# Layer 1's graph visits: products with zeros between TensorE's sums, and lane numbers read from SBUF

## The chip, the cores and the metric

One core of one Trainium2 chip runs the whole program. The metric is the time of one execution in microseconds on the device; the time before is the median of three runs.

## The reference

Two layers of a graph network over 6250 nodes of 256 features and 100000 edges, sorted by their target node `dst`. Layer 1, in which the change lies, computes a graph attention. The core of it, for edges with row = `src` and col = `dst`:

```python
h = (x @ W).reshape(n, 4, 64)
e = leaky_relu((a_l * h).sum(-1)[row] + (a_r * h).sum(-1)[col], 0.2)
ex = exp(e - segment_max(e, row)[row])
att = ex / segment_sum(ex, row)[row]
out = segment_sum(att[:, :, None] * h[col], row)      # (n, 256)
```

Around it stand layer norms, a linear attention and a mixture of experts, which the change does not touch.

## The kernel before

The nodes are tiled by 128 (49 tiles). The edges, sorted by the node that they are summed into, are cut into chunks of 128; a *visit* is one chunk for one tile of nodes. Layer 1 has 880 visits in 110 groups of eight (U = 8). The code is unrolled, with an own list of instructions for each engine; semaphores alone order them.

For each visit POOL gathers 128 rows of `h1_table` (264 numbers each) with one indirect DMA (L534). There are R = 4 slots of eight visits; before each half group of four, POOL waits until PE has summed the visits whose slot it refills (`gnn_ps`). For a group g, in this order:

- DVE compares lane numbers with the node of each edge (`one_hot`, L2088, 128 x 1024, into bf16); the lane numbers of all groups but the first two come from PSUM bank 7 (`lanes_ps`), into which L2131 copied them from `iota`.
- PE transposes the eight one-hots into bank 0 (`flip_hot`, L2168), ACT copies them out (L2037), PE looks up the numbers of the target nodes with them (`look_up`, L2177). ACT widens the one-hots to float32 (L2041).
- DVE makes the scores in four short steps (`attend` stages 0 to 3, the last L2109), ACT takes the exponential (L2045, L2046), DVE multiplies the gathered rows by it in two halves (stages 5 and 6, L2120).
- PE multiplies the one-hot of each visit with its rows (L2196, 128 x 260 float32, banks 4 to 6 in turn) and DVE adds the bank to the tile's sum in SBUF (`add_sums`, L548). PE's sum of visit n waits until DVE has added visit n - 3.

The program order ties the groups together. DVE does the eight adds of group g and, behind each of the last seven, one stage of group g + 1. PE does the look-ups of g + 1, then the sums of g, with the transposes of g + 2 between the fourth and the fifth sum. ACT does the exponentials of g + 1, the copy of the transposed one-hots of g + 2, and widens those of g + 2 when the sums of g are over.

`zeros` is a 128 x 128 float32 tile of zeros in SBUF that other stages use already; `xres` holds the residual of all nodes.

In layer 0, the stretches 440 to 780 and 840 to 1400 us below run visits of their own (gather L534, sum L1216 of 256 columns, add L548) beside other work of PE, DVE and ACT.

Of the kernel before, what the change touches and what calls it, by code (L numbers as in the profile page):

```python
# [16 lines left out]
P = 128  # L17
NODES, D, EDGES = 6250, 256, 100000
# [86 lines left out]
def gps_two_layers(nc, x, src, dst, edge_weight, L0_gnn_W, L0_gnn_b, L0_mix_Wq, L0_mix_Wkv, L0_mix_Wproj,  # L105
# [4 lines left out]
    with ExitStack() as ctx:  # L110
        def sem(name):
            return ctx.enter_context(nc.semaphore(name))
# [18 lines left out]
        def take(words):  # L131
            at = place["at"]
            place["at"] = at + words
            assert place["at"] <= place.get("end", arena_words), place
            return arena[:, at:at + words]
# [4 lines left out]
        xres = take(T * D)  # L140
        ident, tri, ones, iota = take(P), take(P), take(P), take(P)
        zeros, no_edges = take(P), take(2 * SPAN)
# [26 lines left out]
        def bank(b, width=512, at=0):  # L169
            return ps[:, b * 512 + at:b * 512 + at + width]  # L170

        def half(b, i, width=D):
            return ps[:, b * 512 + i * 256:b * 512 + i * 256 + width]

        V, G = Steps(nc.vector, sem("dve_step")), Steps(nc.gpsimd, sem("pool_step"))
# [361 lines left out]
        def load_tiles(engine, first):  # L537

            return nc.values_load_multi_w_load_instructions(
                tile_row[0:1, ds(first, U)], engines=[engine.engine], min_val=0, max_val=T,  # L540
                skip_runtime_bounds_check_because="a visit's tile is a count of at most T tiles")[1]

        def add_sums(dve, n, tile, width, b, sums_before, adds_before):

            dve.wait_ge(gnn_ps, n + (sums_before + 1))
            dve.wait_ge(gnn_add, n + adds_before)
            to = acc[:, ds(tile * ACC_W, width)]
            dve.tensor_tensor(to, to, bank(b, width), ALU.add).then_inc(gnn_add, 1)  # L548
# [1452 lines left out]
        scratch(FREE)  # L2001
        hot = take(2 * U * P).rearrange("p (b u n) -> p b u n", b=2, u=U)
        assert place["at"] <= arena_words - KD * P - SLOT_W
        lanes_ps = bank(7, P)
        ex_ps = bank(1, U * GH).rearrange("p (u h) -> p u h", u=U)
        lc3 = lc.rearrange("p (t w) -> p t w", w=2 * GH)
        rl3 = rl_all.rearrange("p (t w) -> p t w", w=2 * GH)
# [12 lines left out]
        with nc.Block() as block:  # L2020
# [42 lines left out]
            @block.vector  # L2063
            def _(dve):

                V.then(dve.tensor_reduce(r_max, rl3[:, 0:T, 0:GH].rearrange("p t h -> p h t"), AX_X, ALU.max))
                dve.tensor_copy(r_rows.rearrange("p (h n) -> p h n", h=GH),
                                r_max.unsqueeze(2).to_broadcast([P, GH, P])).then_inc(rm_done, 1)
                dve.wait_ge(rm_ps, 1)
                V.then(dve.tensor_reduce(r_max, bank(7, GH * P).rearrange("p (h n) -> p h n", h=GH), AX_X, ALU.max))  # L2070
                dve.sem_inc(rm_done, 1)
                V.then(dve.memset(lc, 0.0))
                V.add(dve.tensor_copy(lc3[:, 0:T, 0:GH], rl3[:, 0:T, GH:]))
                bound = lc3[:, 0:T, GH:]
                V.then(dve.tensor_tensor(bound, rl3[:, 0:T, GH:], r_max.unsqueeze(1).to_broadcast([P, T, GH]), ALU.add))
                V.then(dve.scalar_tensor_tensor(bound, bound, ALPHA, bound, ALU.mult, ALU.max))
                V.then(dve.tensor_scalar(bound, bound, -LIFT - OTHER, None, ALU.add))
                for q in range(PARTS):
                    V.then(dve.tensor_copy(lcp[:, :, q, :], lc3))
                    if q + 1 < PARTS:  # L2080
                        V.then(dve.tensor_tensor(lc3, lc3, lcp[:, :, q, :], ALU.subtract))
                V.then(dve.tensor_copy(ident_b, ident))
                dve.sem_inc(lc_done, 1)
                dve.sem_inc(gnn_add, GNN1_BANKS)

                def one_hot(g, b, lanes):
                    wide = [P, U, P]
                    dve.tensor_tensor(hot_b[b].rearrange("p (u n) -> p u n", u=U), lanes.unsqueeze(1).to_broadcast(wide),  # L2088
                                      v_loc[:, ds(g * U, U)].unsqueeze(2).to_broadcast(wide), ALU.is_equal
                                      ).then_inc(hots_done, 1)  # L2090

                def attend(g, stage):

                    r, b = g % R, g % 2
                    if stage == 0:
                        dve.wait_ge(rows_done[r], g // R * (16 * U) + (ROWS_BEFORE[r] + 16 * U))
                        dve.wait_ge(look_ps, g + 1)
                        V.add(dve.tensor_reduce(look, bank(2 + b, U * LW).rearrange(
                            "p (u q w) -> p u w q", u=U, q=PARTS), AX_X, ALU.add))
                    elif stage == 1:  # L2100
                        V.settle()
                        V.add(dve.tensor_tensor(score, look[:, :, 0:GH], rows[r][:, :, D:D + GH], ALU.add))
                    elif stage == 2:
                        V.settle()
                        V.add(dve.scalar_tensor_tensor(score, score, ALPHA, score, ALU.mult, ALU.max))
                    elif stage == 3:
                        V.settle()

                        dve.scalar_tensor_tensor(score, look[:, :, GH:], OTHER, score, ALU.add, ALU.subtract  # L2109
                                                 ).then_inc(score_done, 1)  # L2110
                    elif stage == 4:
                        if g + 2 < GROUPS1:
                            dve.wait_ge(hot_done32, g + 1)
                            one_hot(g + 2, b, lanes_ps)
                    else:
                        dve.wait_ge(ex_done, g + 1)
                        q = (stage - 5) * HALF_U
                        msg = rows[r][:, q:q + HALF_U, 0:D].rearrange("p u (h f) -> p u h f", h=GH)
                        ex = ex_ps[:, q:q + HALF_U, :].unsqueeze(3).to_broadcast([P, HALF_U, GH, GF])
                        dve.tensor_tensor(msg, msg, ex, ALU.mult).then_inc(msg_done, 1)  # L2120

                STAGES = 7

                for g in range(2):
                    one_hot(g, g, iota)
                for c in range(LOOPS):
                    dve.wait_ge(mx_ps, c + 1)
                    a = xres[:, c * B * D:(c + 1) * B * D]
                    dve.tensor_tensor(a, a, half(4 * (c % 2), 0, B * D), ALU.add).then_inc(mx_add, 1)
                dve.wait_ge(mx_add, LOOPS)  # L2130
                V.then(dve.tensor_copy(lanes_ps, iota))  # L2131
                dve.wait_ge(edges_ready, 2)
                for stage in range(STAGES):
                    attend(0, stage)
                for g in range(GROUPS1):
                    tiles = load_tiles(dve, g * U)
                    for u in range(U):
                        add_sums(dve, g * U + u, tiles[u], ACC_W, 4 + (g * U + u) % GNN1_BANKS, SUMS_BEFORE + R * U,
                                 ADDS_BEFORE + GNN1_BANKS)
                        if u >= U - STAGES and g + 1 < GROUPS1:  # L2140
                            attend(g + 1, u - (U - STAGES))
                dve.wait_ge(gnn_add, NVIS + NVIS1 + GNN0_BANKS + GNN1_BANKS)

            @block.tensor
            def _(pe):
# [4 lines left out]
                for c in range(LOOPS):  # L2150
# [4 lines left out]
                    for n, i in enumerate(group_tiles(c)):  # L2155
                        for k in range(KD):
                            last = pe.matmul(half(4 * (c % 2), n)[:, k * P:(k + 1) * P],
                                             xt_tile(i)[:, k * P:(k + 1) * P], kvm[:, k * P:(k + 1) * P],
                                             start=True, stop=True)
# [24 lines left out]
                for g in range(GROUPS1):  # L2184
                    r, b = g % R, g % 2
                    if g + 1 < GROUPS1:
                        look_up(g + 1, 1 - b)
                    pe.wait_ge(hot_done32, g + 1)
                    pe.wait_ge(den_in, g + 1)
                    for u in range(U):  # L2190
                        if u % HALF_U == 0:
                            pe.wait_ge(msg_done, g * 2 + (u // HALF_U + 1))
                        if u == HALF_U and g + 2 < GROUPS1:
                            flip_hot(g + 2, b)
                        pe.wait_ge(gnn_add, g * U + (ADDS_BEFORE + u + 1))
                        pe.matmul(bank(4 + (g * U + u) % GNN1_BANKS, ACC_W), hot[:, b, u, :], rows[r][:, u, 0:ACC_W],  # L2196
                                  start=True, stop=True).then_inc(gnn_ps, 1)


        W_E = KD * F1  # L2200
# [641 lines left out]
```

## Time and profile before

| what | us |
|---|---|
| median of 3 runs | 4209.23 |
| lowest and highest run | 4208.39, 4214.93 |
| span of the profiled execution, first to last instruction | 4207.4 |
| TensorE's mean granted clock, share of full speed | 0.776 |
| the visits of layer 1, from about | 2107 |
| to about | 3462 |

No other time of the profiled execution is recorded than its span. Engines are named as in the profile: PE is TensorE, PEld its weight loads, DVE VectorE, ACT ScalarE, POOL GpSimd. A matmul on float32 data shows as two records, each with its weight load. PEclk is the clock granted to PE as a share of full speed, 1.0 for 2.4 GHz and 0.5 for 1.2 GHz. "issue" is time in which an engine waited for nothing that the profile shows, and "remote" stands for a releaser that it can't assign to an instruction.

### The profile page before, as it was taken

What the parts mean: (1) busy time and instruction counts of PE and PEld (TensorE: products, weight loads), DVE (VectorE), ACT (ScalarE), POOL (GpSimd) and SP (SyncE); (2) the same over time, 40 slices, a digit from 0 to 9 for tenths busy, and PEclk for the clock granted to TensorE, in tenths of its full rate; (3) what the DMA queues carried; (4) which work ended last, traced back from release to release, by engine and by line L of the source; (5) the groups of instructions that cost most, each with busy time, mean ns of one, the idle gap of its engine ahead of it and who ended that gap; (6) DMA issues with size and microseconds to landing.
All of it is one profiled execution on the core that took longest, in us unless ns stands there. A gap on an engine that the chain in (4) does not pass through costs nothing. (4 is left out here: it accounts for less than half of the span.)

```text
span 4207.4 us, 47856 instructions
## 1 busy us (share of the span) xinstructions
PE 2730.2 (65%) x12850; PEld 2053.4 (49%) x12850; DVE 2571.9 (61%) x5963; ACT 1421.0 (34%) x4306; POOL 2199.0 (52%) x2162
## 2 busy tenths in 40 slices
PE   5476777577777653815666666666666655699984
PEld 4243444355555543614544444444444435599972
DVE  5346998677777786435455565556555567544438
ACT  6663000077777731113221111111111113333334
POOL 0466777666666602573256665666665641255530
PEclk9778887788989865957777777777777775699985
DMA  5332333233333223622223333333333354222234
GB/s 145 87 87 82 89 88 87 86 87 93 89 93 95 86 67 87 159 62 66 69 78 86 91 87 85 87 89 89 89 87 86 87 79 159 76 72 70 71 92 145
DMA packets 204009, 379.38 MB, mean 90 GB/s; under 512 B 48926, under 2 KB 131873, under 8 KB 203619
## 3 DMA queue, kind: packets, MB, share of 16 engines
q0 software_dynamic: 102192, 279.12, 24.7%
q1 hardware_dynamic: 101556, 97.19, 7.5%
q8 instruction: 113, 1.85, 0.2%
q14 instruction: 148, 1.21, 0.1%
HBM read 314.12 MB, written 62.05 MB: 89 GB/s over the span
## 5 line engine op out<-in xcount | busy, mean ns | idle before, releaser
L534 POOL DMA_INDIRECT arena<-h_table,arena x1712 | 1729.3, 1010 | 1082.5 <-issue 479.2
L548 DVE TENSOR_TENSOR arena<-arena,ps 128x260 f32 (+1 forms) x1712 | 719.3, 420 | 848.1 <-remote 355.2
L2196 PE MATMUL ps<-arena 128*128 128x260 f32 x1760 | 674.2, 527 | 376.2 <-DVE arena L548 162.2
L1216 PE MATMUL ps<-arena 128*128 128x256 f32 x1664 | 556.6, 451 | 243.4 <-DVE arena L548 133.3
L2196 PEld LDWEIGHTS ps<-arena 128*128 128x128 f32 x1760 | 411.7, 258 | 534.5 <-issue 249.7
L1216 PEld LDWEIGHTS ps<-arena 128*128 128x128 f32 x1664 | 326.6, 221 | 400.1 <-issue 237.5
L717 ACT ACTIVATE arena<-arena 128x112 f16<-128x112 f16 x1568 | 446.7, 375 | 94.5 <-DVE arena L983 77.9
L2045 ACT ACTIVATE ps<-arena 128x32 f32<-128x32 f32 x110 | 22.1, 201 | 1036.9 <-DVE arena L2109 909.5
L884 DVE TENSOR_SCALAR arena<-arena 128x128 f32<-128x128 f32 x832 | 289.5, 349 | 0.4
L2120 DVE TENSOR_TENSOR arena<-arena,ps 128x1024 f32<-128x1024 f32 x220 | 267.1, 1214 | 2.1 <-ACT ps L2045 2.1
L2570 ACT ACTIVATE arena<-ps,arena 128x128 f32<-128x128 f32 x456 | 143.6, 366 | 307.1 <-PE ps L2618 274.6
L2618 PEld LDWEIGHTS ps<-arena 128*128 128x128 f32 x1824 | 222.8, 192 | 9.1 <-DVE arena L2577 3.4
L2618 PE MATMUL ps<-arena 128*128 128x128 f32 x1824 | 223.6, 276 | 2.6 <-DVE arena L2577 2.6
L2639 PE MATMUL ps<-arena 128*128 x912 | 215.6, 379 | 0.0
L580 ACT ACTIVATE arena<-arena 128x98 bf16<-128x98 f32 (+2 forms) x441 | 188.1, 432 | 77.4 <-remote 44.8
L2177 PE MATMUL ps<-arena 128*128 x880 | 128.6, 192 | 123.5 <-ACT arena L2037 76.8
L2266 POOL DMA_INDIRECT arena<-xn_table,arena x114 | 124.7, 1094 | 148.7 <-DVE arena L2492 101.1
L2557 POOL DMA_INDIRECT y_rows<-arena x114 | 114.8, 1007 | 163.5 <-DVE arena L2601 146.1
L1306 POOL DMA_INDIRECT arena<-xn_table,arena x84 | 81.4, 969 | 216.0 <-DVE arena L1559 160.3
L2177 PEld LDWEIGHTS ps<-arena 128*128 128x128 bf16 x880 | 88.6, 101 | 212.2 <-issue 183.9
L702 ACT ACTIVATE arena<-ps 128x256 f32<-128x256 f32 x98 | 37.3, 380 | 418.7 <-PE ps L1115 230.1
L2639 PEld LDWEIGHTS ps<-arena 128*128 128x128 f32 x912 | 164.5, 190 | 17.7
(525 smaller groups left out, 4486.5 us busy)
## 6 DMA issues: line engine op xcount, KB each, us to landing
arena<-h_table,arena POOLq DMA_INDIRECT x1712
arena<-in_L_ffn_w SPq DMA_DIRECT2D x32, 512.0 KB, 7.7
xn_table<-arena SPq DMA_DIRECT2D x14, 896.0 KB, 4.0
slot_out<-arena SPq DMA_DIRECT2D x21, 512.0 KB
arena<-y_rows SPq DMA_DIRECT2D x12, 896.0 KB, 9.5
h_table<-arena SPq DMA_DIRECT2D x7, 924.0 KB
h_table<-arena SPq DMA_DIRECT2D x7, 896.0 KB, 4.2
arena<-in_x SPq DMA_DIRECT2D x48, 128.0 KB
```

Of the source, the lines that this page charges most:

```text
L534: pool.indirect_dma_start(slot[:, 0:width], None, table, bass.IndirectOffsetOnAxis(ap=idx, axis=0)).then_inc(done, 16)
L548: dve.tensor_tensor(to, to, bank(b, width), ALU.add).then_inc(gnn_add, 1)
L580: act.activation(to, key, ACT.Sign, bias=edge_hi[:, b:b + 1], scale=-1.0, accum_out=out).then_inc(hist_done, 1)
L717: last = act.activation(codes[b][:, c, k, :], slots_[b][:, c, :], ACT.Copy, scale=code_f[k][:, at:at + 1])
L884: dve.tensor_scalar(hot_w[:, g % 2, u, :], iota, v_loc[:, n:n + 1], v_w[:, n:n + 1], ALU.is_equal, ALU.mult).then_inc(hot_done, 1)
L1216: pe.matmul(bank(n % V0_BANKS, D), hot_w[:, g % 2, u, :], rows[:, n % RING, :], start=True, stop=True).then_inc(gnn_ps, 1)
L2120: dve.tensor_tensor(msg, msg, ex, ALU.mult).then_inc(msg_done, 1)
L2177: last = pe.matmul(bank(2 + b, LW, u * LW), hot_t[:, u * P:(u + 1) * P], lc_parts[:, ds(tiles[u] * LW, LW)], start=True, stop=True)
L2196: pe.matmul(bank(4 + (g * U + u) % GNN1_BANKS, ACC_W), hot[:, b, u, :], rows[r][:, u, 0:ACC_W], start=True, stop=True).then_inc(gnn_ps, 1)
L2570: act.activation(h_t[b][:, f * P:(f + 1) * P], bank(2 + 2 * b + f // 2, P, f % 2 * P), ACT.Relu, bias=b1_t[:, ds(experts[b] * FB + f, 1)]) ...
L2618: last = pe.matmul(bank(2 + 2 * b + f // 2, P, f % 2 * P), w1_ring[b][:, k * F1 + f * P:k * F1 + (f + 1) * P], x_t[b][:, k * P:(k + 1) * P ...
L2639: last = pe.matmul(bank(6 + b, D), h_t[b][:, f * P:(f + 1) * P], w2_all[:, ds(experts[b] * W_E + f * D, D)], start=(f == 0), stop=(f == FB ...
```

## The change

Behind the sum of every visit of layer 1, PE gets one more product: `zeros` with the first 256 columns of `xres`, float32, into bank 7, without a wait and without a semaphore. Nobody reads the result. Since bank 7 held the lane numbers of `one_hot`, these are now read from `iota` in SBUF for all groups, and the copy into the bank goes.

```diff
-        lanes_ps = bank(7, P)
         ex_ps = bank(1, U * GH).rearrange("p (u h) -> p u h", u=U)
...
                         if g + 2 < GROUPS1:
                             dve.wait_ge(hot_done32, g + 1)
-                            one_hot(g + 2, b, lanes_ps)
+                            one_hot(g + 2, b, iota)
...
                 dve.wait_ge(mx_add, LOOPS)
-                V.then(dve.tensor_copy(lanes_ps, iota))
                 dve.wait_ge(edges_ready, 2)
...
                         pe.matmul(bank(4 + (g * U + u) % GNN1_BANKS, ACC_W), hot[:, b, u, :], rows[r][:, u, 0:ACC_W],
                                   start=True, stop=True).then_inc(gnn_ps, 1)
+                        pe.matmul(bank(7, D), zeros, xres[:, 0:D], start=True, stop=True)
```

## Rows read from the trace of the kernel before

**Rows 1.** The page: busy time of each engine over the whole span.

```profile
PE 2730.2 (65%) x12850; PEld 2053.4 (49%) x12850; DVE 2571.9 (61%) x5963; ACT 1421.0 (34%) x4306; POOL 2199.0 (52%) x2162
```

**Rows 2.** The last step of the softmax (L2109): times, first and last start.

```profile
L2109 DVE SCALAR_TENSOR_TENSOR arena<-arena x110: 185/186/247, 2108.2 to 3451.9; 128x32 f32<-128x32 f32 x110
```

**Rows 3.** Stretches: length, busy us (count) of PE, PEld, DVE, ACT, POOL, clock, DMA.

```profile
440.00:780.00 340.00, 242.28 (x692) 140.78 (x691) 297.20 (x676) 25.87 (x84) 270.77 (x228) 0.81 0.31 88
840.00:1400.00 560.00, 401.80 (x2149) 318.45 (x2148) 415.72 (x1107) 431.86 (x1516) 355.33 (x342) 0.88 0.32 91
2107.00:3436.00 1329.00, 834.34 (x3429) 563.91 (x3430) 767.22 (x1604) 241.45 (x429) 803.94 (x848) 0.72 0.34 87
```

**Rows 4.** Waits of 2107 to 3465: who, for whom, us, times, longest.

```profile
DVE arena L548 <- remote: 283.8, 75, 8.4
DVE arena L548 <- PE ps L2196: 211.2, 273, 2.9
DVE arena L548 <- issue: 40.3, 74, 7.3
...
POOL arena L534 <- PE ps L2196: 269.1, 110, 27.9
```

**Rows 5.** Timeline of DVE around a long wait: start, us, what, idle before.

```profile
2634.75 0.43 DVE L548 TENSOR_TENSOR arena<-arena,ps 128x260 f32 x1 [0.56 <-PE ps L2196]
...
2636.90 0.43 DVE L548 TENSOR_TENSOR arena<-arena,ps 128x260 f32 x1 [1.62 <-PE ps L2196]
...
2644.68 0.43 DVE L548 TENSOR_TENSOR arena<-arena,ps 128x260 f32 x1 [7.25 <-remote]
```

**Rows 6.** Timeline of PE in the same stretch.

```profile
2633.88 0.61 PE L2168 MATMUL ps<-arena 128*128 128x128 bf16 x8
2634.32 0.66 PE L2196 MATMUL ps<-arena 128*128 128x260 f32 x2
...
2637.38 0.71 PE L2196 MATMUL ps<-arena 128*128 128x260 f32 x2 [1.44 <-issue]
2645.16 1.24 PE L2196 MATMUL ps<-arena 128*128 128x260 f32 x2 [7.07 <-DVE arena L548]
```

**Rows 7.** Timeline of POOL there.

```profile
2641.29 0.95 POOL L534 DMA_INDIRECT arena<-h_table,arena  x1 [0.30 <-issue]
2647.19 0.94 POOL L534 DMA_INDIRECT arena<-h_table,arena  x1 [4.95 <-PE ps L2196]
```

**Rows 8.** Short stretches: behind another long wait, and the last two full groups.

```profile
2713.30:2717.50 4.20, 3.56 (x14) 2.89 (x15) 2.48 (x8) 0.00 (x0) 1.23 (x2) 0.50 0.01 2
...
3436.60:3444.40 7.80, 7.16 (x35) 4.59 (x33) 7.07 (x16) 2.30 (x4) 0.00 (x0) 0.86 0.38 34
3444.40:3451.90 7.50, 6.05 (x23) 4.31 (x23) 6.18 (x16) 2.19 (x4) 0.00 (x0) 0.81 0.00 0
```

**Rows 9.** Groups of instructions, 2000 to 3700: busy us, mean ns, idle before.

```profile
L2196 PE MATMUL ps<-arena 128*128 128x260 f32 x1760 | 674.2, 527 | 376.2 <-DVE arena L548 162.2 <-issue 157.8 <-DVE arena L2120 50.6
...
L2120 DVE TENSOR_TENSOR arena<-arena,ps 128x1024 f32<-128x1024 f32 x220 | 267.1, 1214 | 2.1 <-ACT ps L2045 2.1
L2088 DVE TENSOR_TENSOR arena<-ps,arena 128x1024 bf16<-128x1024 f32 x108 | 131.5, 1218 | 0.0
```

**Rows 10.** PE's sums back to back, at the full and at the half clock.

```profile
2703.46 0.82 PE L2196 MATMUL ps<-arena 128*128 128x260 f32 x3
...
2716.36 1.07 PE L2196 MATMUL ps<-arena 128*128 128x260 f32 x2
```

**Rows 11.** Single lines: ns shortest/median/longest.

```profile
L1216 PE MATMUL ps<-arena x466: 377/381/767, 440.5 to 779.9; 128*128 128x256 f32 x156
...
L2088 DVE TENSOR_TENSOR arena<-arena x2: 1222/1224/1226, 2054.8 to 2055.9; 128x1024 bf16<-128x1024 f32 x2
```

**Rows 12.** Timeline of the two comparisons with numbers from SBUF.

```profile
2054.75 2.37 DVE L2088 TENSOR_TENSOR arena<-arena 128x1024 bf16<-128x1024 f32 x2 [0.25 <-issue]
2055.63 1.17 POOL L534 DMA_INDIRECT arena<-h_table,arena  x1 [0.30 <-issue]
```

## The prediction

> **What bounds the kernel now.** I read the lanes of the page first, then the waits and the timeline of the stretch that the change touches. The page says that no engine is full over the span [rows 1], so the question is what sets the pace of this one stage, the 110 groups of eight visits in layer 1. The first step 3 of `attend` starts at 2108.2 us and the last at 3451.9 us [rows 2], so a group takes 1343.7 / 109 = 12.33 us. Against that stand the engines' own times. POOL needs 0.95 us for a gather and 0.30 us behind it [rows 7], 10.0 us for eight. From 2107 to 3436, 1329 us or 107.8 groups, DVE is busy 767.22 us, 7.1 us per group, and PE 834.34 us, 7.7 us [rows 3]. None fills 12.33 us. The waits tell where the rest goes: POOL waits 269.1 us for PE's sums, 2.45 us per group, and 10.0 + 2.45 is the group's time. It waits because its ring of four slots is full. DVE waits 283.8 us for something that the profile can't name ("remote"), in 75 pieces, 211.2 us for PE and 40.3 us for issue, 4.9 us per group together [rows 4].
>
> The 75 pieces decide. In the timeline [rows 5 to 7] the sum that PE starts at 2634.32, behind eight transposes, is over by 2634.98. DVE adds it at 2644.68, 9.7 us later, and has added nothing since 2637.33, while POOL goes on gathering until 2642.24. POOL then has nothing to do for 4.95 us until PE's sums free a slot. Where the gathers are over, in the last two full groups, the same instructions take 7.80 and 7.50 us [rows 8]. So a group is: DVE's own chain of about 7.5 to 8 us, and 4 to 5 us in which PE's finished work isn't seen by DVE, and this only while POOL gathers without a pause. The add at 2636.90 comes 2.15 us after the one before, the next 7.78 us later; the first step is one sum of two matmul records, the second eight transposes and a sum, ten records. That is 0.8 to 1.1 us for a record. It looks as if PE's work were reported one record at a time and slowly in these pieces, but the trace doesn't show why.
>
> The granted clock over the stage is 0.72 [rows 3], so PE is at the lower of its two levels for 2 x (1 - 0.72) = 56% of the time.
>
> **The change, part by part.** *The zero matmuls.* 880 more instructions in the code, one behind each sum, each of 256 float32 columns. A sum of 260 columns shows as two records (1760 for 880 visits [rows 9]), so there are 1760 more records and as many weight loads. The price is not in the trace of this stage, but its neighbour is: at the full clock three records in a row take 0.82 us, the last 0.38, so one starts 0.22 us after the other; at the half clock two take 1.07 us, the last 0.64, so 0.43 us [rows 10]. A record of 256 columns in layer 0 takes 377 ns at its shortest [rows 11], as good as the same. So a zero product costs 2 x 0.22 = 0.43 us at 2.4 GHz and 2 x 0.42 = 0.85 us at 1.2 GHz, 3.5 or 6.8 us for a group. PE idles 12.33 - 7.7 = 4.6 us per group, so the work fits at the full clock. What hides it is the time in which PE waits anyway for an add (three banks of sums, so PE is at most three sums ahead) and for DVE's two multiplications of 1.21 us at the end of the group [rows 9]. At the full clock a sum and its zeros, 0.87 us, are slower than DVE's add with a small step of the softmax, 0.43 + 0.19 us with their gaps, for sums 4 and 5 alone: some 0.1 to 0.3 us per group without cover.
>
> *Half clock behind a stall.* After such a piece PE stands at the lower level: at 2645.16 one pair takes 1.24 us [rows 6], and the clock from 2713.3 to 2717.5, behind another, is 0.50 [rows 8]. I count all 75. There a zero product of 0.85 us stands in the way of one sum or none before DVE's long operations cover it again: 0 to 0.85 us, I take the middle, 0.4 us x 75 = +30 us. The 0.1 to 0.3 us of the full clock I leave in the interpolation below, which contains it.
>
> *What the clock gives back.* More work between the sums makes the lower level rarer. DVE waits for PE 273 times [rows 4]. A sum at the full clock comes 0.43 us sooner. If the share at the lower level is halved, that is 273 x 0.43 x 0.28 = 33 us; bounds: nothing, and all 211.2 us.
>
> *The weights in front.* Each zero product loads `zeros`, and each sum after it its own one-hot again. The loads lie beside the matmuls: the three records at 0.22 us from start to start [rows 10] have a load in front of each. Nothing.
>
> *More records to report.* This is the term that I think decides. A group has 16 records of sums, 8 of transposes and 8 of look-ups, 32; with the change 48. If the "remote" time goes by records, it grows by half: 283.8 x 0.5 = +142 us, the upper bound. If it ends when POOL's ring is full whatever PE does, as at 2642.24, it stays: +0. Between them I go by three stretches with the same gathers and other numbers of PE records [rows 3]: layer 0 from 440 to 780 has 692 / 228 x 8 = 24 records for eight gathers and 340 / 228 = 1.49 us per gather; this stage 32 and 1329 / 848 = 1.57 us; layer 0 from 840 to 1400 has 50 and 560 / 342 = 1.64 us. From 32 to 48 that is 0.07 x 16 / 18 = 0.062 us per visit, x 880 = +55 us. The three differ in much else, so this is an estimate.
>
> *Lanes from SBUF.* 108 comparisons from the bank take 1218 ns [rows 9], the two from SBUF 1224 ns [rows 11]: 108 x 6 ns = +0.7 us, and one copy of 128 columns goes. The gather that began in the middle of those two took 1.17 instead of 0.95 us [rows 12]. At worst 0.22 us x 108 = 24 us of POOL, which has 269.1 us of waiting to hide it in; if that cover is gone, it shows in full. I take 0. The Trainium skill (SBUF — State Buffer, Who interferes with whom) says that a DVE instruction with two SBUF inputs contends with a GpSimd instruction that reads SBUF, and infers that descriptor generation isn't hit. By the stronger reading each comparison could hold POOL for its whole 1.2 us, 108 times; the row of 1.17 us allows a fifth of that.
>
> Sum: 55 + 30 - 33 = +52 us on a span of 4207.4 us. The span is the profiled execution's whole record; it lies 1.8 us below the median of the runs, 4209.23 us, so the prediction is 4261 us. A difference of 0.2%, 8 us, is what a measurement of this kernel can tell from none.
>
> **The rivals.** *The clock wins.* PE stays at the upper level, its sums are there when DVE asks, and the pieces without reports get shorter as PE never rests. For it: 162.2 + 157.8 us of idle time before PE's sums [rows 9], and the level 0.50 after a stall [rows 8]. Against: the stalls are 5 to 8 us of waiting that zeros between sums can't fill, since PE is three sums ahead and stops. The gain is half of DVE's 211.2 us, -105 us, 4104 us; with the whole of it and some of the remote time up to -200 us. It decides if the remote time doesn't grow with the records. The Trainium skill (TensorE: Matmul & The Clock Gate, HAM oscillation) says that gaps between matmul bursts bring the half clock back and that a kernel without them gains. By that rule alone the outcome would be this rival.
>
> *Nothing to see.* The zeros lie in PE's idle time, the remote time ends with POOL's ring, and POOL's 10.0 + 2.45 us stand: 4209 +- 8 us. For it speaks that POOL paces the group; against it that there are 16 new records between what DVE waits for.
>
> *PE becomes the bound.* At the lower level a group costs PE 8 x 0.86 us for sums, 6.8 for zeros and twice the 0.61 of the full clock for the transposes [rows 6], 14.9 us. If the lower level keeps its 56%, the loss is 0.56 x (14.9 - 12.33) x 110 = +158 us, 4367 us. Against it: PE that has been busy for a while gets the upper level back: transposes at the upper level stand at 2633.88 [rows 6] in the middle of a dense group, so the state ends itself.
>
> **How the numbers follow.** Forecast case 0.52 (4261 us, its own range 4222 to 4348: 30% of the 55 us give 16 + 30 - 33 = +13, the upper bound of the records gives 142 + 30 - 33 = +139). The clock wins 0.25, nothing 0.15, PE bound 0.08. The range is to leave out no more than the far end of the clock's gain, below 4120, and what lies above PE's bound, a tenth each at most: 4120 to 4370 us. Slower 0.52 + 0.08 = 0.60; same 0.15; faster 0.25.
>
> **What would show it.** Right: between two steps of the softmax 12.8 us on average; the new matmul with 1760 records; a granted clock above 0.8 in the stage and yet DVE's "remote" wait above 283.8 us; POOL's gathers still at 0.95 us. Wrong: "remote" smaller than before with a higher clock (the clock wins), or the same group time with PE busy 3.5 us more (nothing). If gathers take 1.1 us or more, the lanes in SBUF did it. If PE is busy over 11 us of a group at a clock near 0.6, PE is the bound.

## The result, and the profile after

The changed kernel takes 4337.56 us (median, 4333.24 to 4342.21), the kernel before beside it 4208.81: ratio 1.0311, interval 1.0291 to 1.0332, so 3.1% or 129 us slower. The forecast was slower by 52 us. The profiled execution took 4333.24 us with a span of 4331.5.

The page's busy line, and the last step of the softmax (L2108, which was L2109; shortest, median and longest ns, first and last start), after:

```profile
PE 3014.0 (70%) x14610; PEld 2381.7 (55%) x14610; DVE 2572.7 (59%) x5962; ACT 1425.8 (33%) x4306; POOL 2241.4 (52%) x2162
```

```profile
L2108 DVE SCALAR_TENSOR_TENSOR arena<-arena x110: 185/186/257, 2108.1 to 3573.2; 128x32 f32<-128x32 f32 x110
```

PE has 1760 records more, as foreseen, and 284 us more work. The stage starts at the same 2108 us as before [rows 2] and ends 121 us later: 1465.1 / 109 = 13.44 us for a group instead of 12.33. So nearly the whole loss arises between the first and the last of these starts. The same three stretches as in [rows 3]:

```profile
440.00:780.00 340.00, 242.33 (x688) 144.52 (x686) 295.98 (x674) 24.96 (x81) 270.53 (x229) 0.80 0.31 89
840.00:1400.00 560.00, 397.01 (x2162) 314.27 (x2163) 419.57 (x1120) 436.48 (x1536) 356.71 (x345) 0.90 0.32 91
2107.00:3436.00 1329.00, 1014.24 (x4713) 797.32 (x4713) 703.55 (x1473) 226.66 (x396) 782.07 (x780) 0.81 0.29 80
```

Layer 0 is as before. In layer 1 the clock is up from 0.72 to 0.81, and in the same 1329 us POOL does 780 gathers where it did 848. The groups of instructions (2000 to 3800; busy us, mean ns, idle time before them), for [rows 9]:

```profile
L534 POOL DMA_INDIRECT arena<-h_table,arena x880 | 880.8, 1001 | 702.9 <-PE ps L2194 289.3 <-issue 249.0 <-remote 83.4
L2194 PE MATMUL ps<-arena 128*128 128x260 f32 x1760 | 641.9, 451 | 314.0 <-DVE arena L2119 138.1 <-issue 122.6 <-DVE arena L548 48.7
L2196 PE MATMUL ps<-arena 128*128 128x256 f32 x1760 | 603.7, 429 | 0.0
...
L548 DVE TENSOR_TENSOR arena<-arena,ps 128x260 f32 x880 | 374.1, 425 | 686.5 <-remote 330.7 <-PE ps L2194 308.7 <-issue 28.4
...
L2087 DVE TENSOR_TENSOR arena<-arena 128x1024 bf16<-128x1024 f32 x110 | 134.1, 1220 | 0.2 <-issue 0.2
```

Read L548 against [rows 4]: remote 283.8 to 330.7, +47 us; PE 211.2 to 308.7, +98; issue -12. Together DVE idles 123 us more (563.5 to 686.5), the loss of the stage. L534 is new too: a gather takes 1001 ns instead of 949 (the same view of before), 46 us over 880. POOL's own wait for PE is 289.3 us where it was 269.1, so in the sum over the stage its time to spare has not gone.

The means hide a pattern. Here are two neighbouring groups (windows; the columns of [rows 3]), three gathers of POOL around them, and the comparison of DVE that the first of these gathers meets (timeline):

```profile
2228.70:2244.00 15.30, 10.26 (x56) 8.31 (x55) 7.14 (x16) 2.29 (x4) 10.93 (x11) 0.97 0.38 103
2244.00:2256.00 12.00, 10.82 (x41) 8.25 (x42) 7.18 (x16) 2.24 (x4) 5.11 (x5) 0.61 0.19 51
```

```profile
2230.16 1.49 POOL L534 DMA_INDIRECT arena<-h_table,arena  x1 [0.30 <-issue]
...
2241.94 0.94 POOL L534 DMA_INDIRECT arena<-h_table,arena  x1 [0.30 <-issue]
2246.18 1.34 POOL L534 DMA_INDIRECT arena<-h_table,arena  x1 [3.29 <-PE ps L2194]
```

```profile
2229.62 1.22 DVE L2087 TENSOR_TENSOR arena<-arena 128x1024 bf16<-128x1024 f32 x1
```

One group at the full clock with 11 gathers and a long wait of DVE, one near the half clock with 5 gathers in which PE is busy 10.8 of 12 us. I took the granted clock of each of the 109 intervals from one L2108 to the next: 54 lie below 0.8 (13.3 us, 5.6 gathers), 55 above (13.6 us, 10.0 gathers), and they change places 107 times, so they alternate throughout. Before, 76 lay below and 33 above, with 63 changes. The two waits of DVE are split between the two kinds: of its 308.7 us for PE, 230 lie in the 54 intervals below 0.8, and of its 330.7 us "remote", 250 lie in the 55 above.

DVE and PE in the second of the two groups (timeline):

```profile
2243.67 0.43 DVE L548 TENSOR_TENSOR arena<-arena,ps 128x260 f32 x1 [6.59 <-remote]
...
2245.49 1.22 DVE L2087 TENSOR_TENSOR arena<-arena 128x1024 bf16<-128x1024 f32 x1
...
2251.51 0.43 DVE L548 TENSOR_TENSOR arena<-arena,ps 128x260 f32 x1 [1.29 <-PE ps L2194]
```

```profile
2244.15 1.23 PE L2194 MATMUL ps<-arena 128*128 128x260 f32 x2 [4.77 <-DVE arena L548]
...
2250.28 1.07 PE L2194 MATMUL ps<-arena 128*128 128x260 f32 x2
2251.14 1.06 PE L2196 MATMUL ps<-arena 128*128 128x256 f32 x2
2252.00 1.07 PE L2194 MATMUL ps<-arena 128*128 128x260 f32 x2
2252.86 0.87 PE L2196 MATMUL ps<-arena 128*128 128x256 f32 x2
2253.57 0.60 PE L2194 MATMUL ps<-arena 128*128 128x260 f32 x2
```

DVE waits 6.59 us for a releaser that the profile can't name. PE has stood for 4.77 us and comes back at the lower level, where sum and zeros take 1.72 us from sum to sum (2250.28 to 2252.00); now DVE waits for PE. The granted clock is 1.00 from 2226.1 to 2243.1, 0.50 from 2243.3 to 2253.3 and 1.00 again from 2253.5 to 2270.3. The two slow gathers, 1.49 and 1.34 us, both start inside a comparison (L2087 at 2229.62 and at 2245.49).

### The profile page after: what moved, and what is told of

Read it like the earlier page. It is cut to its first block and busy times, and to the rows that moved or that the text cites. A ratio compares the mean times of both kernels' runs of the same rounds, so it can differ in the third digit from the quotient of the medians.

```text
span 4331.5 us, 51375 instructions
## 1 busy us (share of the span) xinstructions
PE 3014.0 (70%) x14610; PEld 2381.7 (55%) x14610; DVE 2572.7 (59%) x5962; ACT 1425.8 (33%) x4306; POOL 2241.4 (52%) x2162
## 5 line engine op out<-in xcount | busy, mean ns | idle before, releaser
L534 POOL DMA_INDIRECT arena<-h_table,arena x1712 | 1773.9, 1036 | 1152.1 <-issue 478.0
L548 DVE TENSOR_TENSOR arena<-arena,ps 128x260 f32 (+1 forms) x1712 | 720.2, 421 | 992.5 <-remote 417.0
L2194 PE MATMUL ps<-arena 128*128 128x260 f32 x1760 | 641.9, 451 | 314.0 <-DVE arena L2119 138.1
L1216 PE MATMUL ps<-arena 128*128 128x256 f32 x1664 | 550.9, 450 | 240.0 <-DVE arena L548 133.1
L2196 PE MATMUL ps<-arena 128*128 128x256 f32 x1760 | 603.7, 429 | 0.0
L2194 PEld LDWEIGHTS ps<-arena 128*128 128x128 f32 x1760 | 364.0, 221 | 396.4 <-issue 255.4
L1216 PEld LDWEIGHTS ps<-arena 128*128 128x128 f32 x1664 | 329.7, 222 | 388.1 <-issue 220.0
L2196 PEld LDWEIGHTS ps<-arena 128*128 128x128 f32 x1760 | 386.9, 220 | 77.0
L2617 PEld LDWEIGHTS ps<-arena 128*128 128x128 f32 x1824 | 225.2, 194 | 9.1 <-DVE arena L2576 3.3
L2638 PE MATMUL ps<-arena 128*128 x912 | 215.7, 380 | 0.0
L2556 POOL DMA_INDIRECT y_rows<-arena x114 | 114.1, 1001 | 167.2 <-DVE arena L2600 149.8
L2638 PEld LDWEIGHTS ps<-arena 128*128 128x128 f32 x912 | 164.7, 191 | 17.7
```

What stands on the lines that cost most here:

```text
L534: pool.indirect_dma_start(slot[:, 0:width], None, table, bass.IndirectOffsetOnAxis(ap=idx, axis=0)).then_inc(done, 16)
L1216: pe.matmul(bank(n % V0_BANKS, D), hot_w[:, g % 2, u, :], rows[:, n % RING, :], start=True, stop=True).then_inc(gnn_ps, 1)
L2196: pe.matmul(bank(7, D), zeros, xres[:, 0:D], start=True, stop=True)
L2617: last = pe.matmul(bank(2 + 2 * b + f // 2, P, f % 2 * P), w1_ring[b][:, k * F1 + f * P:k * F1 + (f + 1) * P], x_t[b][:, k * P:(k + 1) * P ...
L2638: last = pe.matmul(bank(6 + b, D), h_t[b][:, f * P:(f + 1) * P], w2_all[:, ds(experts[b] * W_E + f * D, D)], start=(f == 0), stop=(f == FB ...
```

## The experiments

The experiments ran in five series. The kernel before did not take the same time in all of them: 4204.66 and 4214.15 us in the first and the last, 3662.91, 3658.64 and 3660.97 in the three between. Each ratio below is to before on the same chip in the same series. I call them long and short series; the measurement of the change was a long one. The expectations speak of a chip with or without remote waits instead, but the chip with number 6 served a series of each kind. What sets the kind I don't know.

### Long series: the halves, narrow zeros, zeros in one piece

**Lanes alone** (e1_lanes).

```diff
-                        pe.matmul(bank(7, D), zeros, xres[:, 0:D], start=True, stop=True)
```

(against the changed kernel: `one_hot` reads `iota`, no zero products)

> Half of the change alone: the lane numbers of all comparisons come from iota in SBUF, and there are no zero products. By the theory that the lanes slow POOL, each of the two or so gathers that lie beside a comparison takes about 1.3 us instead of 0.95, the group pays 0.3 to 0.4 us, and the time is 20 to 48 us above the kernel before (1.005 to 1.011). By my prediction, which took nothing for this part, the ratio is 1.000 within 0.2%, either because gathers are not slowed or because POOL's wait for PE (269.1 us in the kernel before) shrinks by what they lose.

Measured 0.9987 (0.9969 to 1.0006): gathers as the first theory said, time as the second.

```profile
L534 POOL DMA_INDIRECT arena<-h_table,arena x880 | 883.3, 1004 | 573.0 <-issue 257.9 <-PE ps L2194 181.9 <-SPq L2019 80.9
...
L548 DVE TENSOR_TENSOR arena<-arena,ps 128x260 f32 x880 | 374.5, 426 | 548.9 <-remote 284.4 <-PE ps L2194 196.6 <-issue 31.7
```

The gathers are slowed just as in the changed kernel, 1004 ns, and POOL's wait for PE is 182 us instead of 269 [rows 4]: the cover that the prediction named holds here. 156 gathers meet a comparison and take 1260 ns on average, the other 724 take 948; in the kernel before 132 meet one and take 950.

**Zeros alone** (e2_zeros). The bank of look-ups that PE used for this group is free by then, so the lanes can stay in bank 7.

```diff
+                        pe.matmul(bank(2 + b, D), zeros, xres[:, 0:D], start=True, stop=True)
```

> The other half alone: the zero product of 256 columns stands behind every sum, but goes to the look-up bank that is not in use, and the lane numbers stay in PSUM. If the zeros are the cause, the groups alternate as in the changed kernel and the time is 80 to 125 us above the kernel before (ratio 1.019 to 1.030). If the lanes are, the ratio is below 1.005. The prediction's terms without the lanes give 52 us, 1.012.

Measured 1.0041 (1.0027 to 1.0055), 17 us, so that neither half alone explains the change.

```profile
L548 DVE TENSOR_TENSOR arena<-arena,ps 128x260 f32 x880 | 374.1, 425 | 580.2 <-PE ps L2196 371.3 <-remote 140.9 <-issue 43.1
```

```profile
2331.70:2343.90 12.20, 10.17 (x54) 7.77 (x53) 7.24 (x17) 2.29 (x4) 7.58 (x8) 1.00 0.32 89
2343.90:2355.50 11.60, 9.17 (x50) 7.14 (x49) 7.06 (x17) 2.19 (x4) 7.01 (x8) 1.00 0.33 93
```

This is the opposite of the term that I thought decides: with half as many records again per group, the remote wait halves, 283.8 to 140.9. The waits for PE grow by 160. The clock from 2107 to 3436 is 0.90, and groups with eight gathers each follow one another at 1.00; the intervals lie above 0.8 in 89 of 109 cases and change places 37 times.

**Narrow zeros** (e3_narrow).

```diff
-                        pe.matmul(bank(2 + b, D), zeros, xres[:, 0:D], start=True, stop=True)
+                        pe.matmul(bank(2 + b, 8), zeros, xres[:, 0:8], start=True, stop=True)
```

> As the run with zeros alone, but each zero product has 8 columns instead of 256: as many records and weight loads (1760), and hardly any time of PE. Theory records (the prediction's largest term): slow reporting goes by records, so the time is within 20 us of the run with wide zeros. Theory stream (PE busy at the half clock behind a stall is what costs): the time is within 25 us of the kernel before, or somewhat above, since a weight load of 128 columns is left in each.

Measured 1.0046 (1.0024 to 1.0067), as both theories allowed, so it doesn't tell them apart by time.

```profile
L2196 PE MATMUL ps<-arena 128*128 128x260 f32 x1760 | 852.1, 581 | 202.1 <-DVE arena L548 75.6 <-DVE arena L2120 64.4 <-issue 59.3
...
L2198 PEld LDWEIGHTS ps<-arena 128*128 128x128 f32 x1760 | 473.1, 269 | 116.7
L548 DVE TENSOR_TENSOR arena<-arena,ps 128x260 f32 x880 | 374.1, 425 | 581.7 <-PE ps L2196 392.1 <-remote 118.7 <-issue 28.6
L2198 PE MATMUL ps<-arena 128*128 128x8 f32 x1760 | 319.4, 255 | 0.0
```

The clock is 0.70 here. A record of a narrow product takes 255 ns, about as long as the load of its weights, 269 ns; that the load is what it costs is my reading and wasn't tested by a run of its own. The sums, at the lower clock, take 581 ns where they took 435 beside wide zeros.

**Zeros in one piece** (e4_end): eight of the products of e2_zeros behind the last sum of the group.

```diff
+                        if u == U - 1:
+                            for _ in range(U):
+                                pe.matmul(bank(2 + b, D), zeros, xres[:, 0:D], start=True, stop=True)
```

> As the run with zeros alone, but the eight zero products of a group stand together behind its last sum. Theory stream: PE has the same work, but now it lies in one piece of 3.5 us (full clock) to 6.8 us (half clock) where the next group's look-ups and first sum wait for it; the sums after a stall are no longer spread apart. It costs 0 to 60 us if the piece lies in the time in which PE waits for DVE's multiplications, and as much as the spread zeros or more (100 us and up) if PE's total work at the half clock is what counts. Theory records: the same as the spread zeros, 1.02 to 1.03.

Measured 1.0262 (1.0232 to 1.0292), 115 us.

```profile
L548 DVE TENSOR_TENSOR arena<-arena,ps 128x260 f32 x880 | 374.1, 425 | 679.2 <-remote 516.8 <-PE ps L2196 119.1 <-DVE arena L548 17.6
```

The same work of PE as in e2_zeros, at nearly the same clock (0.87), takes 96 us longer, and as remote waits, 516.8 us. So neither the number of records nor PE's busy time prices the zeros; when they stand relative to the rest does.

### Short series: the same kernels without remote waits

**Both halves, zeros in the look-up bank** (e5_both, r2_both, s3_both): e2_zeros with `one_hot(g + 2, b, iota)`.

> The whole change, but the zero products go to the look-up bank that is not in use instead of bank 7. The halves measured alone gave 0.999 (lanes) and 1.004 (zeros in this same bank), the change 1.031. Theory interaction: the two halves together are what costs, so the ratio is 1.025 to 1.035. Theory bank: bank 7 is what costs, so the ratio is 1.000 to 1.008.

> Both halves with the zeros in the look-up bank, again. Theory interaction: on a chip with long remote waits 1.025 to 1.035, the same as the changed kernel beside it. Theory bank: on such a chip at most 1.008. On a chip without them 1.0095.

> Both halves, zeros in the look-up bank. On a chip with remote waits: theory interaction 1.025 to 1.035; theory bank at most 1.008. On one without 1.010, as twice measured.

Measured 1.0095, 1.0111 and 1.0092, each +-0.0017. The question of the long series isn't answered by them.

**The changed kernel** (r1_change), **lanes alone** (s1_lanes), **zeros alone** (s2_zeros).

> The changed kernel itself, beside the three below on one chip. The first four runs were on a chip where the kernel before takes 4205 us and DVE has long remote waits, the next four on one where it takes 3663 us and has none. On a chip of the first kind the ratio is 1.031, as in the measurement of the change. On one of the second kind POOL's gathers alone set the pace and those beside a comparison from SBUF are slower: 0.04 us x 880 = 35 us, 1.0095, as in the run with both halves and the zeros in the look-up bank.

> Lanes from SBUF alone, again. On a chip without DVE's remote waits (before: 3660 us) POOL's gathers set the pace, and all that they lose shows: 0.04 us x 880 = 35 us, ratio 1.0095, all of what the change costs there (1.0104). On a chip with them (before: 4205 us) 0.999 as before.

> Zeros alone (in the unused look-up bank), again. On a chip without remote waits PE has 3 us to spare in a group of 10 us and the clock is up: ratio 1.000 within 0.2%. On a chip with them 1.004.

Measured 1.0104 (1.0087 to 1.0121), 1.0081 (1.0063 to 1.0100) and 1.0010 (1.0001 to 1.0020). The changed kernel from 1820 to 2890: window, gathers, DVE's longest sum of waits before its adds.

```profile
1820.00:2890.00 1070.00, 955.82 (x5050) 754.19 (x5051) 750.24 (x1579) 233.11 (x420) 813.91 (x827) 0.99 0.39 105
```

```profile
L534 POOL DMA_INDIRECT arena<-h_table,arena x827 | 815.3, 986 | 256.4 <-issue 231.2 <-PE ps L2194 25.2
```

```profile
DVE arena L548 <- PE ps L2194: 39.2, 90, 1.3
```

The same window with zeros alone:

```profile
1820.00:2890.00 1070.00, 967.07 (x5164) 768.73 (x5164) 764.64 (x1609) 238.57 (x428) 805.33 (x851) 0.99 0.41 108
```

There is no remote wait, and with zeros alone POOL makes 851 gathers in the 1070 us, almost without a pause: 0.95 + 0.30 us per gather, 10 us a group. DVE's longest wait is here for the gathered rows, 229 us in the changed kernel. Now POOL is the bound, its cover is gone, and the lanes show in full: 986 ns against 948 with zeros alone, 38 x 880 = 33 us, of 35 measured. With zeros the clock of this window is 0.99, with lanes alone 0.85, and it buys nothing.

**POOL slower without lanes** (e6_pool_slower, r4_pool_slower).

```diff
                     gather_row(pool, rows[r][:, u, :], ROW1, v_idx[:, n:n + 1], h1_table, rows_done[r])
+                    if n % U == 1:
+                        G.then(pool.memset(pause, 0.0))
```

> The run with zeros alone (1.004), lanes in PSUM, and in each group POOL fills a small tile once, behind the second gather, and waits for the end of it: some 0.4 to 0.8 us per group, as much or somewhat more than the comparisons from SBUF take from its gathers (0.31 to 0.44 us). Theory interaction by POOL's pace: the time jumps as in the changed kernel, ratio 1.02 and above. Theory that it is the place of the slow gathers (beside the comparison) or DVE's own reads that counts: the ratio stays at 1.000 to 1.010.

> Zeros alone and POOL slower by one small fill per group, again. On the chip without remote waits it gave 1.012, POOL's own time in full. On a chip with them: theory interaction by POOL's pace 1.02 and above; theory place (only gathers slowed beside the comparison matter) 1.000 to 1.010.

Measured 1.0119 and 1.0120, each +-0.0017: a POOL that loses some 0.4 us per group loses it in the time too. In a long series it wasn't run.

**A pause behind every fourth gather** (e9_pause): the kernel before with the same fill at `n % HALF_U == HALF_U - 1`.

> The kernel before, and behind every fourth gather POOL fills a small tile and waits for its end, a pause of some 0.5 us from gathering, 1 us per group. Theory A (unbroken gathering holds PE's reports back): the long waits of DVE nearly go, and the group is POOL's 10.0 us and 1 us of pauses, up to 1.3 us less than the 12.33 us of before: 0.97 to 0.99. Theory B: POOL's group is 1 us longer, half of it hidden in its wait for PE: 1.00 to 1.02.

Measured 1.0560 (1.0542 to 1.0577), a miss for both.

```profile
2205.08 0.96 POOL L534 DMA_INDIRECT arena<-h_table,arena  x1 [0.30 <-issue]
2206.34 0.95 POOL L534 DMA_INDIRECT arena<-h_table,arena  x1 [0.31 <-issue]
2207.29 0.41 POOL L2034 MEMSET arena<- 128x352 f32 x1
2208.51 0.95 POOL L534 DMA_INDIRECT arena<-h_table,arena  x1 [0.82 <-POOL arena L2034]
```

From gather to gather 2.17 instead of 1.25 us, so a pause costs 0.92 and the group 1.84; x110 = 202 of the 206 us. I had put a pause at 0.5. The same fill costs only some 0.4 us in e6_pool_slower, where it stands behind the second gather; why its place counts wasn't tested. Since the series was a short one, the run says nothing of theory A or B.

**A wait before each gather** (e8_before_waits, r3_waits, s4_waits). In the kernel before, POOL waits for four sums before every fourth gather.

```diff
-                        if n >= R * U:
-                            pool.wait_ge(gnn_ps, n + (SUMS_BEFORE + HALF_U))
-                        elif n % U == 0 and r:
+                        if n < R * U and n % U == 0 and r:
                             pool.wait_ge(mx_ps, -(-r * SLOT_W // (B * D)))
                         pool.sem_inc(dma_turn, 1)
+                    if n >= R * U:
+                        pool.wait_ge(gnn_ps, n + (SUMS_BEFORE + 1))
```

> The kernel before, but POOL waits for a sum before each gather instead of for four sums before every fourth. Nothing else is changed. In the trace of before, DVE's long waits begin only where POOL has gathered five times or more without a pause. Theory A (PE's finished sums are reported late while POOL gathers without a pause): POOL now stops as soon as it is one gather ahead of the reported sums, so pieces end sooner and the time falls by 20 to 150 us (0.965 to 0.995), with remote below 200 us. Theory B (the long waits come with the half clock or with the number of PE's records, whatever POOL does): within 0.3% of before.

> The kernel before with a wait of POOL before each gather, again; on the chip without remote waits it gave 1.000. Theory A (reports are held back while POOL gathers without a pause): on a chip with remote waits 0.965 to 0.995. Theory B (they don't depend on POOL): within 0.3% of before.

> The kernel before with a wait of POOL before each gather. On a chip with remote waits: theory A (reports are held back while POOL gathers without a pause) 0.965 to 0.995; theory B (they don't depend on POOL) within 0.3% of before. On one without 1.000, as twice measured.

Measured 0.9998, 0.9998 and 0.9993, each +-0.001. The stage of the last (L2109):

```profile
L2109 DVE SCALAR_TENSOR_TENSOR arena<-arena x110: 184/185/208, 1819.7 to 2904.3; 128x32 f32<-128x32 f32 x110
```

Where there are no remote waits, the finer wait is free and useless.

### Long series again: the two that were open

> Both halves, zeros in the look-up bank, once more. On a chip with remote waits (before: 4205 us): theory interaction 1.025 to 1.035, theory bank at most 1.008. On one without (before: 3660 us) 1.009 to 1.011, as three times measured.

> The kernel before with a wait of POOL before each gather, once more. On a chip with remote waits: theory A (reports held back while POOL gathers without a pause) 0.965 to 0.995; theory B (they don't depend on POOL) within 0.3% of before. On one without 1.000, as three times measured.

**s5_both** measured 1.0275 (1.0246 to 1.0304), +116 us, with the pattern of the changed kernel: 54 intervals below 0.8 and 55 above, 107 changes of place.

```profile
L534 POOL DMA_INDIRECT arena<-h_table,arena x880 | 880.7, 1001 | 704.3 <-PE ps L2194 282.8 <-issue 251.5 <-remote 88.7
...
L548 DVE TENSOR_TENSOR arena<-arena,ps 128x260 f32 x880 | 374.2, 425 | 685.5 <-remote 332.5 <-PE ps L2194 295.6 <-issue 34.6
```

Line by line the changed kernel's. The bank isn't the cause. The halves alone gave -0.1% and +0.4% in a long series; together they give 2.8 to 3.1%.

**s6_waits** measured 0.9807 (0.9773 to 0.9841), which is 81 us below before. Its stage (L2109), the waits of DVE and of POOL, and POOL's timeline:

```profile
L2109 DVE SCALAR_TENSOR_TENSOR arena<-arena x110: 185/186/250, 2099.6 to 3366.4; 128x32 f32<-128x32 f32 x110
```

```profile
DVE arena L548 <- PE ps L2196: 219.5, 240, 3.4
DVE arena L548 <- remote: 210.5, 71, 4.0
...
POOL arena L534 <- remote: 116.5, 66, 2.7
```

```profile
2381.48 0.94 POOL L534 DMA_INDIRECT arena<-h_table,arena  x1 [1.96 <-remote]
...
2386.76 0.94 POOL L534 DMA_INDIRECT arena<-h_table,arena  x1 [0.59 <-PE ps L2196]
...
2393.17 0.94 POOL L534 DMA_INDIRECT arena<-h_table,arena  x1 [1.71 <-remote]
```

POOL now pauses mostly after four gathers (115 such stretches without a pause of over 0.4 us; before 42, and 37 of eight and 25 of twelve). DVE's remote waits are as many as before, 71 to 75, but the longest is 4.0 instead of 8.4 us and their sum 210.5 instead of 283.8. The stage is 1266.8 us long, 77 shorter. Theory A's range of the ratio holds; its "remote below 200" was missed by 10. The remote waits in this kernel hang on how POOL's gathers are paced. The edit does two things at once, and they weren't run apart: POOL stops within a half group, and it may also start one as soon as a single row is free instead of four. Its waits for PE and "remote" together are about as long as before (285.6 us against 292.4), but come in 302 pieces instead of 119. This version beats both kernels in the long series, and costs nothing in the short ones.

## Why the prediction was off, by its own steps

**What bounds the kernel.** Right in its rows, and the doubt at its end was due: POOL's pacing sets the length of the long waits (s6_waits). One reading went too far: the 4 to 5 us of a group in which PE's finished work "isn't seen" are all of DVE's waits, and the remote ones are 283.8 / 110 = 2.6 us of them. Not seen from one trace: in the short series the same instructions have no remote waits.

**More records to report, +55 us (0 to +142): the term I leaned on, and its sign is wrong.** With the zeros alone the remote waits fell by 143 us; with 8 zeros in one piece they rose by 233. Records don't price them. The three stretches from which I interpolated, 1.49, 1.57 and 1.64 us per gather, differ in much else, as the text said, and the else was it.

**Lanes from SBUF, 0 (at worst 24 us): the step that failed.** Measured, each gather that meets a comparison takes 1.28 us instead of 0.95, some 144 of them: 48 us of POOL, twice the bound. I had taken one gather for each comparison, and its price from the single one of 1.17 us [rows 12]. That gather did not meet the middle of the comparisons but the last 0.34 us of the first (2054.75 + 1.22 - 2055.63), and a gather loses about what is left of the comparison in which it starts. In the changed kernel 98 start inside one, with 0.62 us of it left on average, and lose 0.49 us; four with 1.12 us left lose 0.99; the 46 that were already running when a comparison began lose nothing.

Where POOL is the bound the lanes cost 28 us alone (s1_lanes), most of the 35 us of the whole change (r1_change); in a long series alone nothing (0.9987), as the cover held. But in company with the zeros they are the difference between 1.004 and 1.0275 to 1.031. The prediction expected them to show when POOL's cover is gone; here they cost most while POOL still waits 289.3 us for PE, so time to spare in the sum over the stage did not hide them. Adding parts one by one could not find this: the sum of the halves is +12 to +16 us (by the ratios or by the medians), both together +116 to +129.

The Trainium skill (SBUF — State Buffer, Who interferes with whom) names this pair of instructions. Its inference that descriptor generation isn't hit can't be carried to a whole gather, which is slowed here, in the descriptors or in reading its row numbers; no row tells which. The stronger reading, a hold for the instruction's whole time, comes close for gathers that start inside a comparison (0.99 us lost with 1.12 us left) and fails for those that were running before it (nothing lost).

**Half clock behind a stall, +30 us, and the clock gives back -33.** The mechanism was right, the size was not. DVE's waits for PE went up by 98 us, not down: in the low stretch shown above sums come 1.72 us apart until the clock is up again, and 230 of the 308.7 us lie in such intervals. In the changed kernel the granted clock rose to 0.81 as forecast (above 0.8), yet the time at the lower level fell only from 56% to 38%, and a visit there is twice the work.

**The rivals.** "PE becomes the bound" comes near in the group shown, PE busy 10.82 of 12.00 us at 0.61, where I had said over 11 us near 0.6. Over the 54 intervals below 0.8 PE is busy 10.4 of 13.3 us on average, so it fits many of them and not all. It was rated at 0.08 because PE wins the full clock back; it does, at 2253.5, in the middle of the group, but the clock is at 0.50 again behind 2270.3, beside DVE's next long waits (4.16 and 3.71 us, "remote"). Its sum of 14.9 us also left out the eight look-ups, 1.16 us at the lower level (L2175 at 2246.27), so its 158 us were too low by its own reckoning. "The clock wins" is what the zeros alone do to the clock (0.90) and to the remote waits (half), and it still didn't make the kernel faster: PE's waits took 160 of it. The Trainium skill (TensorE: Matmul & The Clock Gate, HAM oscillation) ties a gain to closed gaps; here the clock rose in every run with wide zeros (from 0.72 to 0.81, 0.87 and 0.90 in the long series; 0.99 in the short ones, against 0.84 in s4_waits), and none was faster.

**What stays open.** Why the slower gathers tip the zeros' even groups (eight gathers each, at the full clock) into the alternation of 11 and 5: POOL's pace or the place of the slow gathers; the run that would tell, POOL slower without lanes, met only short series. And what makes a series long, that is, why PE's finished sums are seen late in it at all.

## What to carry to other kernels

Where two engines are tied by a ring and a few banks, run the parts of a change alone and together before pricing them: here -0.1% and +0.4% made +3.1%. A wait of a producer before every item instead of every fourth keeps it from running ahead in one piece when reports come late; it cost nothing measurable in the short series and gave 1.9% in the long one. Work put on an idle engine to hold its clock is paid at the lower clock after each stall, so end the stall first.

## What the runs showed of the hardware

- A gather's issue on POOL takes 0.95 us, and in the long series 1.26 to 1.29 us on average (up to 1.99, in e1_lanes) when it meets a DVE comparison that reads both inputs from SBUF; beside the same comparison with one input in PSUM it stays at 0.95 (950 ns for 132 of them). The loss is about what is left of the comparison when the gather starts: 0.49 us of 0.62 in the changed kernel (98 gathers), 0.52 of 0.65 in e1_lanes (93); gathers already running when the comparison starts lose nothing (46 and 63).
- The kernel before took 4205 to 4214 us in two series and 3659 to 3663 in three. No trace of it was kept from a short series, but s4_waits has its time there and gathers of the same 0.95 us. Against that trace the one of before has DVE's remote waits in layer 1, 283.8 us against none, and a group of 12.33 us against (2904.3 - 1819.7) / 109 = 9.95 us. It also comes to this stage 288 us later (2108.2 against 1819.7), with remote waits in the stages before it where s4_waits has none, so about half of the difference lies outside the stage.
- A product of 8 columns isn't cheap: with 128 columns of weights each of its two records took 255 ns and each load 269 ns on average at a clock of 0.70, and the time was that of 256 columns (1.0046 and 1.0041).
